# POOL's order of low parts, the place of the router's product on PE, and layer norm statistics by one bn_stats of two tiles

## The chip, the cores and the metric

The kernel runs on one core of a Trainium2 chip. The metric is the device time of one execution in microseconds (us). Engines: PE is TensorE (matmuls; PEld its weight loads), DVE is VectorE, ACT is ScalarE, POOL is GpSimd, SP is SyncE, which here only issues DMAs.

## The reference, cut to what matters

x has 32 batch rows of 512 tokens by 256 channels, all float32. Each row r has six modulation vectors of 256 numbers (sa, ca, ga, sb, cb, gb), made from a conditioning vector.

```python
h = layernorm(x) * (1 + ca) + sa                 # over the 256 channels, eps 1e-5
S = scan over tokens: s = a * s + (1 - a) * h    # a = sigmoid(decay), by channel
x = x + ga * (S @ W.T + b + conv5(h) + conv_b)   # conv5: five taps along tokens, by channel
h = layernorm(x) * (1 + cb) + sb
sel = argmax(gelu(h[:, -1] @ Wp1 + bp1) @ Wp2 + bp2)         # one of 8 experts a row
g = gelu(h @ W1[sel] + b1[sel])
x = x + gb * (h + 0.3 * ((g @ W2[sel] + b2[sel]) @ Wo + bo))
```

## The kernel before, in words

**Tiles.** A row is held as 4 tiles of 128 tokens by 256 channels (`xr`), or, transposed, as 2 tiles of 128 channels by 512 tokens (h, S, rT, hid). The hidden layer of the expert has 4 quarters of 128 features by 512 tokens (g, with f = 0 to 3). For accuracy every large product is made of three: the activation is split into a rounded high part (ACT: `S_hi`, `hid_hi`, `g_hi`) and the remaining low part (POOL: `S_lo`, `hid_lo`, `g_lo`, each one 128x512 subtraction), and the weights likewise; PE does low weight times high part, high times high, high times low part. The products with the high part stand ahead of the product with the low part (`mix`, lines 918, 919, 922; `down`, lines 953, 954, 958; `up`, lines 938 to 940).

**Order.** There is no planner. Each engine has its own list of work, written out by hand as `slot(i)` for i = -3 to 32, and engines meet only by semaphores. An engine does its list strictly in order, so a wait holds up all that stands behind it. Slot i works on four rows at once: row i is in its expert (up, gelu, down), row i+1 in its second norm, hid and router, row i+2 in its mix, convolution and residual, row i+3 in its first norm, h, scan and split of S, and DVE and POOL do the statistics of row i+4. All parts are there in slots 0 to 28 (POOL's and DVE's part for row i+4 in slots up to 27). Setup fills slots -3 to -1: the 8 experts' tables are made there.

**PE's list in a slot** (line 981): mix (line 909) of row i+2, transposes of the slot before's result (line 970), up 0, up 1, transposes of xn, down 0, the first half of up 2, the router's product `nav` (line 1008: four one-column matmuls with Wp1), the second half of up 2, transposes of row i+3 (line 978), the router's logits (lines 1020, 1021), down 1, up 3, transposes of row i+2's residual, down 2, down 3.

**ACT's list** (line 575): two normalisations (line 512; the first writes into S's buffer once both S_lo are made), gelu 0, g_hi 0, gelu 1, g_hi 1 (lines 552, 559), hid (617), hid_hi (625), the router's gelu (634), which waits for PE's nav, rT (572), gelu 2, h (647), g_hi 2, S_hi 0 (546), gelu 3, g_hi 3, S_hi 1, hid_gated (683).

**POOL's list** (line 443): rstd and nmr of the second norm (lines 420, 422), g_lo 0, g_lo 1 (434), gbeta (457), hid_lo (466), rstd and nmr of the first norm of row i+4, g_lo 2, g_lo 3, S_lo 0, S_lo 1 (442).

**DVE's list** (line 784): the expert's result (792), convolution (754, ten instructions) with the last residual in between (803), statistics of row i+4 (`stats1`: four bn_stats, line 704, four bn_aggr, 708, then -mean, 711, and variance + eps, 712), the argmax (832, 834), the scan (781, two), the first residual and statistics of row i+2 (762, 766, 770, 773, 774).

Of the kernel before, what the change touches and what calls it, by code (L numbers as in the profile page):

```python
# [5 lines left out]
def adaln_attention_ffn_kernel(nc, x, decay_logit, W, b, conv_w, conv_b, Wp1, bp1, Wp2, bp2,  # L6
# [16 lines left out]
    ALU = mybir.AluOpType  # L23
    ACT = mybir.ActivationFunctionType

    P = 128
    B, T, D = x.shape
# [4 lines left out]
    TT = T // P  # L32
    DC = D // P
    FC = F // P
    TPB = 512 // D
    HB = TT // TPB
    NX = 6
    NMOD = 6 * D // 512
    EPS = 1e-5
    OUT_SCALE = 0.3  # L40
    GATE_MIN = 0.25

# [19 lines left out]
    with ExitStack() as ctx:  # L62
        def sb(name, shape, dt=f32):
            return ctx.enter_context(nc.sbuf_tensor(name, shape, dt))
# [4 lines left out]
        def sem(name):  # L69
            return ctx.enter_context(nc.semaphore(name))  # L70
# [25 lines left out]


        xr = sb("xr", [P, NX, TT, D])
        st1 = sb("st1", [P, TT, 6])
        mv1 = sb("mv1", [P, TT, 2])  # L100
        ve1 = sb("ve1", [P, TT])
        nm1 = sb("nm1", [P, TT])
        rstd1 = sb("rstd1", [P, TT])
        nmr1 = sb("nmr1", [P, TT])
        st2 = sb("st2", [P, TT, 6])
        mv2 = sb("mv2", [P, TT, 2])
        ve2 = sb("ve2", [P, TT])
        nm2 = sb("nm2", [P, TT])
        rstd2 = sb("rstd2", [P, TT])
        nmr2 = sb("nmr2", [P, TT])  # L110
        xn = sb("xn", [P, TT, D])
# [106 lines left out]
        stored = [sem("stored0"), sem("stored1")]  # L218
        up_loaded = [sem("up_loaded0"), sem("up_loaded1")]
        down_loaded = [sem("down_loaded0"), sem("down_loaded1")]  # L220
        st1_step = sem("st1_step")
        aggr1 = sem("aggr1")
        stats1_ready = sem("stats1_ready")
        rstd1_step = sem("rstd1_step")
        norm1_ready = sem("norm1_ready")
# [9 lines left out]
        r1_ready = sem("r1_ready")  # L235
        t2_done = sem("t2_done")
        x1_ready = sem("x1_ready")
        st2_step = sem("st2_step")
        aggr2 = sem("aggr2")
        stats2_ready = sem("stats2_ready")  # L240
        rstd2_step = sem("rstd2_step")
        norm2_ready = sem("norm2_ready")
# [38 lines left out]
        def wait(eng, s, v):  # L281
            if v > 0:
                eng.wait_ge(s, v)

        def row(r):
            return 0 <= r < B
# [121 lines left out]
        def _(pool):  # L408
# [4 lines left out]
            nc.gpsimd.affine_select(out=ident[:, :], in_=ident[:, :], compare_op=ALU.not_equal, fill=1.0,  # L413
                                    base=0, pattern=[[-1, P]], channel_multiplier=1).then_inc(s_const, 1)

            def norm(r, stats_ready, used, nm, ve, rstd, nmr, step, ready):

                pool.wait_ge(stats_ready, r + 1)
                wait(pool, used, TT * r)
                nc.gpsimd.tensor_tensor(rstd[:, :], ve[:, :], minus_half[:, :], ALU.pow).then_inc(step, 1)  # L420
                pool.wait_ge(step, r + 1)
                nc.gpsimd.tensor_tensor(nmr[:, :], nm[:, :], rstd[:, :], ALU.mult).then_inc(ready, 1)  # L422

            def w1_lo(e):
                pool.wait_ge(s_w1_hi, e + 1)
# [8 lines left out]
                nc.gpsimd.tensor_tensor(g_lo[:, f], g[:, f % 2], g_hi[:, f].bitcast(f32), ALU.subtract).then_inc(g_lo_ready, 1)  # L434

            def norm1(r):
                norm(r, stats1_ready, xn1_ready, nm1, ve1, rstd1, nmr1, rstd1_step, norm1_ready)

            def s_low(r, c):
                wait(pool, mix_done, DC * r)  # L440
# [2 lines left out]

            def slot(i):
                if row(i + 1):
                    norm(i + 1, stats2_ready, xn2_ready, nm2, ve2, rstd2, nmr2, rstd2_step, norm2_ready)
                if i == -3:
                    w1_lo(0)
                if i == -1:
                    w1_lo(5)  # L450
                if row(i):
                    g_low(i, 0)
                    g_low(i, 1)

                    wait(pool, hid_gated_ready, DC * i)
                    pool.wait_ge(up_loaded[i % 2], 16 * (i // 2 + 1))
                    nc.gpsimd.tensor_tensor(gbeta[:, :], up_w[:, i % 2, U_BETA:UPW].bitcast(f32), mods[:, GB:GB + DC, i],
                                            ALU.mult).then_inc(gbeta_ready, 1)
                if row(i + 1):
                    r = i + 1  # L460
                    wait(pool, up_done, FC * (r - 1))
                    if r == 0:
                        pool.wait_ge(s_split_out[0], 32)
                    for c in range(DC):
                        pool.wait_ge(hid_hi_ready, DC * r + c + 1)
                        nc.gpsimd.tensor_tensor(hid_lo[:, r % 2, c], hid_at[r % 2][:, c], hid_hi[:, r % 2, c].bitcast(f32),
                                                ALU.subtract).then_inc(hid_lo_ready, 1)
                if i == -2:
                    w1_lo(3)
                if row(i + 4):  # L470
                    norm1(i + 4)
                if i == -1:
                    w1_lo(6)
                    w1_lo(7)
                if row(i):
                    g_low(i, 2)
                    g_low(i, 3)
                if row(i + 3):
                    s_low(i + 3, 0)
                    s_low(i + 3, 1)  # L480
                if i == -3:
                    w1_lo(1)
                    w1_lo(2)
                if i == -2:
                    w1_lo(4)
# [204 lines left out]
        def _(dve):  # L690
# [7 lines left out]
            dve.wait_ge(s_keep, 1)  # L698
            nc.vector.tensor_scalar(fresh[:, :], keep[:, :], -1.0, 1.0, ALU.mult, ALU.add).then_inc(s_fresh, 1)

            def stats1(r):
                dve.wait_ge(x_loaded[r % NX], 16 * (r // NX + 1))
                for j in range(TT):
                    nc.vector.bn_stats(st1[:, j], xr[:, r % NX, j]).then_inc(st1_step, 1)  # L704
                wait(dve, norm1_ready, r)
                dve.wait_ge(st1_step, TT * (r + 1))
                for j in range(TT):
                    ins = nc.vector.bn_aggr(mv1[:, j], st1[:, j])  # L708
                ins.then_inc(aggr1, 1)
                dve.wait_ge(aggr1, r + 1)  # L710
                nc.vector.tensor_scalar_mul(nm1[:, :], mv1[:, :, 0], -1.0)  # L711
                nc.vector.tensor_scalar_add(ve1[:, :], mv1[:, :, 1], EPS).then_inc(stats1_ready, 1)  # L712

            def mods_setup():

                dve.wait_ge(s_modT, 1)
                view = Q[1][:, 0:6 * DC * B].rearrange("p (m r) -> p m r", r=B)
                nc.vector.tensor_copy(mods[:, SA:SA + DC], view[:, SA:SA + DC])
                nc.vector.tensor_scalar_add(mods[:, CA:CA + DC], view[:, CA:CA + DC], 1.0).then_inc(s_mods1, 1)
                nc.vector.tensor_copy(mods[:, SB:SB + DC], view[:, SB:SB + DC])  # L720
                nc.vector.tensor_scalar_add(mods[:, CB:CB + DC], view[:, CB:CB + DC], 1.0)
                for q, m in enumerate((GA, GB)):
                    ins = nc.vector.tensor_copy(gate_raw[:, q], view[:, m:m + DC])
                ins.then_inc(s_dve, 1)
# [33 lines left out]
            def residual1(r):  # L758
                for k in range(HB):
                    ts = slice(k * TPB, (k + 1) * TPB)  # L760
                    dve.wait_ge(t2_done, HB * r + k + 1)
                    nc.vector.tensor_tensor(xr[:, r % NX, ts], xr[:, r % NX, ts], TR[k][:, :].rearrange("p (t d) -> p t d", d=D),
                                            ALU.add).then_inc(x1_ready, 1)
                    dve.wait_ge(x1_ready, HB * r + k + 1)
                    for j in range(k * TPB, (k + 1) * TPB):
                        nc.vector.bn_stats(st2[:, j], xr[:, r % NX, j]).then_inc(st2_step, 1)
                wait(dve, norm2_ready, r)
                dve.wait_ge(st2_step, TT * (r + 1))
                for j in range(TT):
                    ins = nc.vector.bn_aggr(mv2[:, j], st2[:, j])  # L770
                ins.then_inc(aggr2, 1)
                dve.wait_ge(aggr2, r + 1)
                nc.vector.tensor_scalar_mul(nm2[:, :], mv2[:, :, 0], -1.0)
                nc.vector.tensor_scalar_add(ve2[:, :], mv2[:, :, 1], EPS).then_inc(stats2_ready, 1)

            def scan(r):

# [69 lines left out]
        def _(pe):  # L847
# [74 lines left out]
                        ins = mm(Y[e][:, :], mix_w[:, 0, d, es], S_lo[:, d], start=False, stop=(d == DC - 1))  # L922
                    ins.then_inc(mix_done, 1)

            def up(i, f, parts=range(DC)):
                par, n = i % 2, FC * i + f
                if f == 0:
                    pe.wait_ge(up_loaded[par], 16 * (i // 2 + 1))
                    pe.wait_ge(hid_lo_ready, DC * (i + 1))
                if f == 1:  # L930
                    wait(pe, sel_ready, i + 1)
                if f == 3:

                    pe.wait_ge(sel_ready, min(i + 2, B))
                wait(pe, gelu_out, n - 1)
                for c in parts:
                    w = c * F + f * P
                    mm(U[f % 2][:, :], up_w[:, par, UP + w:UP + w + P], hid_hi[:, par, c], start=(c == 0), stop=False)  # L938
                    mm(U[f % 2][:, :], up_w[:, par, w:w + P], hid_hi[:, par, c], start=False, stop=False)  # L939
                    ins = mm(U[f % 2][:, :], up_w[:, par, w:w + P], hid_lo[:, par, c], start=False, stop=(c == DC - 1))  # L940
                if DC - 1 in parts:
                    ins.then_inc(up_done, 1)

            def down(i, f):
                par, n = i % 2, FC * i + f
# [35 lines left out]
            def slot(i):  # L981
# [13 lines left out]
                    expert(e)  # L995
                if row(i):
                    down(i, 0)
                    up(i, 2, (0,))
                if row(i + 1):
                    r = i + 1  # L1000
                    if r == 0:
# [5 lines left out]
                    for c in range(DC):  # L1007
                        ins = mm(U[1][:, 0:1], wp1[:, c], hid_at[r % 2][:, c, T - 1:T], start=(c == 0), stop=(c == DC - 1))
                    ins.then_inc(r_nav, 1)
                if row(i):  # L1010
                    up(i, 2, (1,))
                if row(i + 3):
                    r = i + 3
                    to_channels(r, xn1, xn1_ready, t1_done)
# [52 lines left out]
```

## Time and profile before

| | us |
|---|---|
| median of 3 runs | 711.05 (710.99 to 711.21) |
| the profiled execution | 709.73 |
| its span, first to last instruction | 707.8 |
| PE busy | 657.7 (93% of the span) |
| PEld busy | 517.2 (73%) |
| DVE busy | 599.8 (85%) |
| ACT busy | 567.2 (80%) |
| POOL busy | 466.8 (66%) |

The profiled execution has 1.93 us around its span. A page of the profile gives busy times, the chain of work that ended last, and the costliest groups of instructions. The timelines give single instructions of one engine by start and duration; the square brackets at a row's end give the time in which the engine stood idle before it and what ended that. Records of successive instructions on one engine overlap a little: the step from start to start is what an instruction costs there, the record's end is what others wait for.

### The profile page before, as it was taken

Reading aid. Unit: us, or ns where it says so; the run is one execution under the profiler, and the core shown is the slowest. Engines: PE = TensorE matmul, PEld = TensorE weight load, DVE = VectorE, ACT = ScalarE, POOL = GpSimd, SP = SyncE. Lnnn points to the kernel's source line nnn. Section 1 sums busy time; section 2 is a strip of 40 time slices with the busy share of each in tenths; the row PEclk is TensorE's granted clock in tenths of the full one; section 3 lists DMA queues with packets and bytes.
Section 4 is the critical chain, followed back from the end, with each engine's and each line's share of the span. In section 5 each row is a group of like instructions: output and inputs, shape, how many; then the busy total and the mean of one; then the engine's idle time right before and its main releaser. Section 6 shows DMA issues by size and latency. Waiting matters only on the chain.

```text
span 707.8 us, 11426 instructions
## 1 busy us (share of the span) xinstructions
PE 657.7 (93%) x3431; PEld 517.2 (73%) x3431; DVE 599.8 (85%) x1350; ACT 567.2 (80%) x979; POOL 466.8 (66%) x432
## 2 busy tenths in 40 slices
PE   5869589999999999999999999999999999999896
PEld 2758367777777778777777777777777777777764
DVE  1778759999999999999999999999999999997621
ACT  3766668888888889988888888889888888887753
POOL 1544556776777776666767777777677777776542
PEclk9989989999999999999999999999999999999998
DMA  7996644555555554454554555545445555544451
GB/s 243 334 298 207 190 143 150 175 179 153 176 162 167 179 160 138 156 151 173 178 176 153 164 163 180 178 132 148 160 161 177 179 155 174 155 143 151 145 158 55
DMA packets 55457, 120.60 MB, mean 170 GB/s; under 512 B 5643, under 2 KB 43364, under 8 KB 46180
## 3 DMA queue, kind: packets, MB, share of 16 engines
q1 hardware_dynamic: 51316, 115.12, 51.7%
q10 hardware_dynamic: 4080, 4.75, 2.3%
q8 instruction: 28, 0.46, 0.3%
q14 instruction: 33, 0.27, 0.1%
HBM read 61.12 MB, written 25.19 MB: 122 GB/s over the span
## 4 chain that ended last, share of the span: by engine, by line
DVE 42%; POOL 25%; PE 15%; issue 8%; ACT 6%; DMA 2%; SPq 0%; POOLq 0%; DVEq 0%; ACTq 0%
DVE Y L754 24%; POOL S_lo L442 9%; POOL g_lo L434 9%; DVE st L704 5%; DVE xr L803 4%; POOL rstd L420 4%; DVE nm L711 3%; PE Y L922 2%; POOL nmr L422 2%; PE Q L905 2%; PE U L938 2%; PE U L940 1%; PE U L939 1%; DVE mv L708 1%; DVE S L781 1%
## 5 line engine op out<-in xcount | busy, mean ns | idle before, releaser
L434 POOL TENSOR_TENSOR g_lo<-g,g_hi 128x512 fp32r<-128x512 f32 x128 | 191.2, 1502 | 162.1 <-ACT g_hi L559 156.5
L754 DVE SCALAR_TENSOR_TENSOR Y<-h,taps,Y 128x512 f32<-128x512 f32 x320 | 222.9, 752 | 13.1 <-PE Y L922 10.6
L512 ACT ACTIVATE S<-xr,nmr,rstd 128x256 f32<-128x256 f32 x128 | 66.6, 592 | 63.9 <-POOL S_lo L442 59.4
L938 PE MATMUL U<-hid_hi,up_w 128*128 128x512 f32 x256 | 107.1, 419 | 7.7 <-DMA up_w<-up_table 7.7
L953 PE MATMUL Q<-g_hi,down_w 128*128 128x512 f32 x256 | 109.7, 429 | 0.2
L552 ACT ACTIVATE g<-U,up_w 128x512 f32<-128x512 f32 x128 | 88.6, 692 | 24.9 <-PE U L940 21.7
L940 PE MATMUL U<-hid_lo,up_w 128*128 128x512 f32 x256 | 101.6, 397 | 0.0
L939 PE MATMUL U<-hid_hi,up_w 128*128 128x512 f32 x256 | 101.5, 397 | 0.0
L954 PE MATMUL Q<-g_hi,down_w 128*128 128x512 f32 x256 | 101.2, 395 | 0.0
L420 POOL TENSOR_TENSOR rstd<-ve,minus_half 128x4 f32<-128x4 f32 x64 | 65.3, 1020 | 30.1 <-DVE ve L712 23.0
L781 DVE TENSOR_TENSOR_SCAN S<-keep,h 128x512 f32<-128x512 f32 x64 | 75.9, 1228 | 10.3 <-ACT h L647 10.3
L958 PE MATMUL Q<-g_lo,down_w 128*128 128x512 f32 x256 | 83.7, 408 | 0.7 <-POOL g_lo L434 0.7
L559 ACT CAST g_hi<-g 128x512 fp32r<-128x512 f32 x128 | 80.5, 629 | 3.1
L442 POOL TENSOR_TENSOR S_lo<-S,S_hi 128x512 fp32r<-128x512 f32 x64 | 81.1, 1288 | 1.9 <-ACT S_hi L546 1.9
L512 ACT ACTIVATE xn<-xr,nmr,rstd 128x256 f32<-128x256 f32 x128 | 66.1, 587 | 9.2 <-POOL nmr L422 9.2
L958 PEld LDWEIGHTS Q<-g_lo,down_w 128*128 128x128 f32 x256 | 45.0, 187 | 23.8 <-POOL g_lo L434 14.6
L922 PE MATMUL Y<-S_lo,mix_w 128*128 128x512 f32 x128 | 47.8, 417 | 14.5 <-POOL S_lo L442 14.5
L938 PEld LDWEIGHTS U<-hid_hi,up_w 128*128 128x128 f32 x256 | 48.8, 191 | 16.7 <-DMA up_w<-up_table 8.1
L792 DVE SCALAR_TENSOR_TENSOR rT<-Q,mods,w_raw 128x512 f32<-128x512 f32 x64 | 44.7, 738 | 17.8 <-PE Q L958 17.8
L940 PEld LDWEIGHTS U<-hid_lo,up_w 128*128 128x128 f32 x256 | 48.7, 190 | 11.4
L953 PEld LDWEIGHTS Q<-g_hi,down_w 128*128 128x128 f32 x256 | 48.1, 188 | 9.9 <-ACT g_hi L559 1.0
L939 PEld LDWEIGHTS U<-hid_hi,up_w 128*128 128x128 f32 x256 | 49.0, 191 | 8.7
(129 smaller groups left out, 1335.7 us busy)
## 6 DMA issues: line engine op xcount, KB each, us to landing
up_w<-up_table SPq DMA_DIRECT2D x32, 1027.0 KB, 6.6
down_w<-down_tab SPq DMA_DIRECT2D x32, 1024.0 KB, 8.6
xr<-in_L_attn_x_dram SPq DMA_DIRECT2D x32, 512.0 KB, 3.6
out_dram<-xr SPq DMA_DIRECT2D x64, 256.0 KB, 2.3
w_raw<-in_L_ffn_W_dram SPq DMA_DIRECT2D x7, 512.0 KB, 5.3
xr<-in_L_ffn_W_dram ACTq DMA_DIRECT2D x6, 512.0 KB, 7.7
up_table<-down_w SPq DMA_DIRECT2D x2, 1024.0 KB, 7.1
up_table<-up_w SPq DMA_DIRECT2D x2, 1024.0 KB, 5.4
```

Of the source, the lines that this page charges most:

```text
L420: nc.gpsimd.tensor_tensor(rstd[:, :], ve[:, :], minus_half[:, :], ALU.pow).then_inc(step, 1)
L434: nc.gpsimd.tensor_tensor(g_lo[:, f], g[:, f % 2], g_hi[:, f].bitcast(f32), ALU.subtract).then_inc(g_lo_ready, 1)
L442: nc.gpsimd.tensor_tensor(S_lo[:, c], S[:, c], S_hi[:, c].bitcast(f32), ALU.subtract).then_inc(S_lo_ready, 1)
L512: nc.scalar.activation(to[:, j], xr[:, r % NX, j], ACT.Identity, bias=nmr[:, j:j + 1], scale=rstd[:, j:j + 1]).then_inc(ready, 1)
L552: nc.scalar.activation(g[:, f % 2], U[f % 2][:, :], ACT.Gelu, bias=up_w[:, i % 2, U_B1 + f:U_B1 + f + 1].bitcast(f32)).then_inc(gelu_out, 1)
L754: ins = nc.vector.scalar_tensor_tensor(out=Y[c][:, :], in0=h[:, c, k:k + T], scalar=taps[:, c, k:k + 1], in1=Y[c][:, :], op0=ALU.mult, op1 ...
L938: mm(U[f % 2][:, :], up_w[:, par, UP + w:UP + w + P], hid_hi[:, par, c], start=(c == 0), stop=False)
L939: mm(U[f % 2][:, :], up_w[:, par, w:w + P], hid_hi[:, par, c], start=False, stop=False)
L940: ins = mm(U[f % 2][:, :], up_w[:, par, w:w + P], hid_lo[:, par, c], start=False, stop=(c == DC - 1))
L953: mm(Q[c][:, :], down_w[:, par, 1, w:w + P], g_hi[:, f], start=(f == 0), stop=False)
L954: mm(Q[c][:, :], down_w[:, par, 0, w:w + P], g_hi[:, f], start=False, stop=False)
L958: ins = mm(Q[c][:, :], down_w[:, par, 0, w:w + P], g_lo[:, f], start=False, stop=(f == FC - 1))
```

## The change

Four edits. On POOL, S_lo 0 moves from behind g_lo 3 to between g_lo 2 and g_lo 3. On PE, up 2 is no longer in two halves: the router's nav product comes behind the whole of it. On DVE, a bn_stats reads two tiles, interleaved channel by channel: its six outputs (count, mean, count x variance of the even and of the odd elements) are then the statistics of the two tiles, so bn_aggr and the two small tensor_scalars go (in the second norm, lines 766 to 774, as in the first). POOL's `norm` does their work instead: 256 x variance + 256 x eps, and -mean, ahead of the power and the product. Its rstd is therefore 1/16 of the old one, and the factor 16 is put into (1 + ca) and (1 + cb) once in setup.

```diff
@@ POOL
-            def norm(r, stats_ready, used, nm, ve, rstd, nmr, step, ready):
-                pool.wait_ge(stats_ready, r + 1)
+            def norm(r, stats_ready, used, st, rstd, nmr, step, ready):
+                pool.wait_ge(stats_ready, HB * (r + 1))
                 wait(pool, used, TT * r)
-                nc.gpsimd.tensor_tensor(rstd[:, :], ve[:, :], minus_half[:, :], ALU.pow).then_inc(step, 1)
-                pool.wait_ge(step, r + 1)
-                nc.gpsimd.tensor_tensor(nmr[:, :], nm[:, :], rstd[:, :], ALU.mult).then_inc(ready, 1)
+                nc.gpsimd.tensor_scalar(rstd[:, :], st[:, :, 2], D * EPS, None, ALU.add).then_inc(step, 1)
+                nc.gpsimd.tensor_scalar(nmr[:, :], st[:, :, 1], -1.0, None, ALU.mult)
+                pool.wait_ge(step, 2 * r + 1)
+                nc.gpsimd.tensor_tensor(rstd[:, :], rstd[:, :], minus_half[:, :], ALU.pow).then_inc(step, 1)
+                pool.wait_ge(step, 2 * r + 2)
+                nc.gpsimd.tensor_tensor(nmr[:, :], nmr[:, :], rstd[:, :], ALU.mult).then_inc(ready, 1)
@@ POOL, slot
                 if row(i):
                     g_low(i, 2)
+                if row(i + 3):
+                    s_low(i + 3, 0)
+                if row(i):
                     g_low(i, 3)
                 if row(i + 3):
-                    s_low(i + 3, 0)
                     s_low(i + 3, 1)
@@ DVE
+            def pair_stats(st, r, k):
+                pair = xr[:, r % NX, k * TPB:(k + 1) * TPB].rearrange("p t d -> p d t")
+                return nc.vector.bn_stats(st[:, k * TPB:(k + 1) * TPB].rearrange("p t s -> p (t s)"), pair)
+
             def stats1(r):
                 dve.wait_ge(x_loaded[r % NX], 16 * (r // NX + 1))
-                for j in range(TT):
-                    nc.vector.bn_stats(st1[:, j], xr[:, r % NX, j]).then_inc(st1_step, 1)
                 wait(dve, norm1_ready, r)
-                dve.wait_ge(st1_step, TT * (r + 1))
-                for j in range(TT):
-                    ins = nc.vector.bn_aggr(mv1[:, j], st1[:, j])
-                ins.then_inc(aggr1, 1)
-                dve.wait_ge(aggr1, r + 1)
-                nc.vector.tensor_scalar_mul(nm1[:, :], mv1[:, :, 0], -1.0)
-                nc.vector.tensor_scalar_add(ve1[:, :], mv1[:, :, 1], EPS).then_inc(stats1_ready, 1)
+                for k in range(HB):
+                    pair_stats(st1, r, k).then_inc(stats1_ready, 1)
...
-                nc.vector.tensor_scalar_add(mods[:, CA:CA + DC], view[:, CA:CA + DC], 1.0).then_inc(s_mods1, 1)
+                nc.vector.tensor_scalar(mods[:, CA:CA + DC], view[:, CA:CA + DC], ROOT_D, ROOT_D, ALU.mult, ALU.add).then_inc(s_mods1, 1)
...
+                    if k == 0:
+                        wait(dve, norm2_ready, r)
                     dve.wait_ge(x1_ready, HB * r + k + 1)
...
+                    pair_stats(st2, r, k).then_inc(stats2_ready, 1)
@@ PE, slot
                 if row(i):
                     down(i, 0)
-                    up(i, 2, (0,))
+                    up(i, 2)
                 if row(i + 1):
...
                         ins = mm(U[1][:, 0:1], wp1[:, c], hid_at[r % 2][:, c, T - 1:T], start=(c == 0), stop=(c == DC - 1))
                     ins.then_inc(r_nav, 1)
-                if row(i):
-                    up(i, 2, (1,))
```

## Rows read from the trace of the kernel before

**Rows 1.** The page: busy time, granted clock by slice, and the chain by engine.

```profile
PE 657.7 (93%) x3431; PEld 517.2 (73%) x3431; DVE 599.8 (85%) x1350; ACT 567.2 (80%) x979; POOL 466.8 (66%) x432
...
PEclk9989989999999999999999999999999999999998
...
DVE 42%; POOL 25%; PE 15%; issue 8%; ACT 6%; DMA 2%; SPq 0%; POOLq 0%; DVEq 0%; ACTq 0%
```

**Rows 2.** Waits from 300 to 500 us: us in total, times, longest us.

```profile
POOL g_lo L434 <- ACT g_hi L559: 44.4, 10, 4.5
ACT S L512 <- POOL S_lo L442: 23.2, 11, 2.3
...
PE Y L922 <- POOL S_lo L442: 5.3, 11, 0.6
PEld Q L958 <- POOL g_lo L434: 5.0, 12, 0.4
```

**Rows 3.** Timeline of PE in one slot: start us, duration us, line and operation.

```profile
633.41 0.50 PE L922 MATMUL Y<-S_lo,mix_w 128*128 128x512 f32 x1 [0.48 <-POOL S_lo L442]
633.75 0.39 PE L918 MATMUL Y<-S_hi,mix_w 128*128 128x512 f32 x1
633.98 0.39 PE L919 MATMUL Y<-S_hi,mix_w 128*128 128x512 f32 x1
...
638.56 0.39 PE L940 MATMUL U<-hid_lo,up_w 128*128 128x512 f32 x1
...
641.76 0.58 PE L1008 MATMUL U<-w_raw,wp 128*128 128x1 f32 x4
642.20 0.48 PE L938 MATMUL U<-hid_hi,up_w 128*128 128x512 f32 x1
...
649.04 0.73 PE L958 MATMUL Q<-g_lo,down_w 128*128 128x512 f32 x2
649.61 0.39 PE L953 MATMUL Q<-g_hi,down_w 128*128 128x512 f32 x1
...
650.55 0.63 PE L958 MATMUL Q<-g_lo,down_w 128*128 128x512 f32 x2
651.01 0.39 PE L918 MATMUL Y<-S_hi,mix_w 128*128 128x512 f32 x1
...
651.93 0.39 PE L922 MATMUL Y<-S_lo,mix_w 128*128 128x512 f32 x1
652.78 0.50 PE L922 MATMUL Y<-S_lo,mix_w 128*128 128x512 f32 x1 [0.46 <-POOL S_lo L442]
```

**Rows 4.** Timeline of ACT in the same slot.

```profile
638.99 0.69 ACT L552 ACTIVATE g<-U,up_w 128x512 f32<-128x512 f32 x1
...
642.61 0.26 ACT L634 ACTIVATE nav<-U,vecs 128x1 f32<-128x1 f32 x1
...
645.99 0.65 ACT L559 CAST g_hi<-g 128x512 fp32r<-128x512 f32 x1
```

**Rows 5.** Timelines of POOL and DVE in the same slot.

```profile
646.78 3.45 POOL L434 TENSOR_TENSOR g_lo<-g,g_hi 128x512 fp32r<-128x512 f32 x2 [1.92 <-ACT g_hi L559]
650.20 2.53 POOL L442 TENSOR_TENSOR S_lo<-S,S_hi 128x512 fp32r<-128x512 f32 x2
...
645.56 2.34 DVE L781 TENSOR_TENSOR_SCAN S<-keep,h 128x512 f32<-128x512 f32 x2 [0.83 <-ACT h L647]
```

**Rows 6.** Timeline of POOL: g_lo 3 of that slot by itself.

```profile
648.95 1.28 POOL L434 TENSOR_TENSOR g_lo<-g,g_hi 128x512 fp32r<-128x512 f32 x1
```

**Rows 7.** Timelines of DVE and POOL in a slot with first norm; its PE starts at 361.82.

```profile
370.41 1.40 DVE L704 BATCH_NORM_STATS2 st<-xr 128x6 f32<-128x256 f32 x4
372.33 0.97 DVE L711 TENSOR_SCALAR nm<-mv 128x4 f32<-128x4 f32 x1
...
370.74 2.54 POOL L466 TENSOR_TENSOR hid_lo<-w_raw,hid_hi 128x512 fp32r<-128x512 f32 x2 [0.40 <-ACT hid_hi L625]
374.54 0.65 POOL L422 TENSOR_TENSOR nmr<-nm,rstd 128x4 f32<-128x4 f32 x1
375.19 3.46 POOL L434 TENSOR_TENSOR g_lo<-g,g_hi 128x512 fp32r<-128x512 f32 x2
```

**Rows 8.** POOL's small instructions: duration ns min/median/max, first and last start us.

```profile
L420 POOL TENSOR_TENSOR rstd<-ve,minus_half x64: 997/1007/1846, 12.7 to 669.9; 128x4 f32<-128x4 f32 x64
L422 POOL TENSOR_TENSOR nmr<-nm,rstd x64: 198/200/942, 13.8 to 671.0; 128x4 f32<-128x4 f32 x64
```

**Rows 9.** Timeline of PE: the first stall of this kind, and a gap near the end.

```profile
109.78 0.50 PE L922 MATMUL Y<-S_lo,mix_w 128*128 128x512 f32 x1 [0.46 <-POOL S_lo L442]
...
671.19 1.09 PE L970 MATMUL Q<-ident,rT 128*128 128x128 f32 x8 [1.78 <-DVE rT L792]
```

More of the change, by code:

```diff
@@ L39, in adaln_attention_ffn_kernel @@
     EPS = 1e-5
+    ROOT_D = 16.0
+    assert ROOT_D * ROOT_D == D
     OUT_SCALE = 0.3
@@ L98, in adaln_attention_ffn_kernel @@
         xr = sb("xr", [P, NX, TT, D])
[L99 to L102, printed above, removed]
+        st1 = sb("st1", [P, TT, 3])
         rstd1 = sb("rstd1", [P, TT])
         nmr1 = sb("nmr1", [P, TT])
[L105 to L108, printed above, removed]
+        st2 = sb("st2", [P, TT, 3])
         rstd2 = sb("rstd2", [P, TT])
@@ L220, in adaln_attention_ffn_kernel @@
         down_loaded = [sem("down_loaded0"), sem("down_loaded1")]
-        st1_step = sem("st1_step")
-        aggr1 = sem("aggr1")
         stats1_ready = sem("stats1_ready")
@@ L237, in adaln_attention_ffn_kernel @@
         x1_ready = sem("x1_ready")
-        st2_step = sem("st2_step")
-        aggr2 = sem("aggr2")
         stats2_ready = sem("stats2_ready")
@@ L436, in norm1 @@
             def norm1(r):
-                norm(r, stats1_ready, xn1_ready, nm1, ve1, rstd1, nmr1, rstd1_step, norm1_ready)
+                norm(r, stats1_ready, xn1_ready, st1, rstd1, nmr1, rstd1_step, norm1_ready)
             def s_low(r, c):
@@ L445, in slot @@
                 if row(i + 1):
-                    norm(i + 1, stats2_ready, xn2_ready, nm2, ve2, rstd2, nmr2, rstd2_step, norm2_ready)
+                    norm(i + 1, stats2_ready, xn2_ready, st2, rstd2, nmr2, rstd2_step, norm2_ready)
                 if i == -3:
@@ L718, in mods_setup @@
                 nc.vector.tensor_copy(mods[:, SA:SA + DC], view[:, SA:SA + DC])
-                nc.vector.tensor_scalar_add(mods[:, CA:CA + DC], view[:, CA:CA + DC], 1.0).then_inc(s_mods1, 1)
+                nc.vector.tensor_scalar(mods[:, CA:CA + DC], view[:, CA:CA + DC], ROOT_D, ROOT_D, ALU.mult, ALU.add).then_inc(s_mods1, 1)
                 nc.vector.tensor_copy(mods[:, SB:SB + DC], view[:, SB:SB + DC])
-                nc.vector.tensor_scalar_add(mods[:, CB:CB + DC], view[:, CB:CB + DC], 1.0)
+                nc.vector.tensor_scalar(mods[:, CB:CB + DC], view[:, CB:CB + DC], ROOT_D, ROOT_D, ALU.mult, ALU.add)
                 for q, m in enumerate((GA, GB)):
@@ L763, in residual1 @@
                                             ALU.add).then_inc(x1_ready, 1)
+                    if k == 0:
+                        wait(dve, norm2_ready, r)
                     dve.wait_ge(x1_ready, HB * r + k + 1)
[L765 to L774, printed above, removed]
+                    pair_stats(st2, r, k).then_inc(stats2_ready, 1)
             def scan(r):
@@ L923, in mix, with up @@
                     ins.then_inc(mix_done, 1)
-            def up(i, f, parts=range(DC)):
+            def up(i, f):
                 par, n = i % 2, FC * i + f
@@ L935, in up @@
                 wait(pe, gelu_out, n - 1)
-                for c in parts:
+                for c in range(DC):
                     w = c * F + f * P
@@ L940, in up @@
                     ins = mm(U[f % 2][:, :], up_w[:, par, w:w + P], hid_lo[:, par, c], start=False, stop=(c == DC - 1))
-                if DC - 1 in parts:
-                    ins.then_inc(up_done, 1)
+                ins.then_inc(up_done, 1)
             def down(i, f):
```

## Prediction, made before the changed kernel was run

> **What bounds the kernel now.** I start with busy shares: PE is busy 93% of the span, DVE 85%, ACT 80%, POOL 66%, and the clock is granted in full through the middle [rows 1]. The kernel repeats one slot. PE's stall for S_lo 1 stands at 109.78, the same stall 28 slots later at 652.78 [rows 3, 9]: 543.00 / 28 = 19.39 us a slot. So I look for what fixes 19.39.
>
> The chain of waits names DVE (42%) and POOL (25%) [rows 1], the engines from which the change takes work or which it reorders. The waits tell more: PE waits only for POOL's low parts (5.3 us in 11 waits for S_lo, its weight loads 5.0 us for g_lo), POOL waits for ACT's g_hi, and ACT waits 2.1 us a slot for S_lo [rows 2]. The deciding view is the slot from 633.41 to 652.78. It is slot 28, where no row is left for DVE's first statistics and POOL's first norm. It still lasts 19.37 us. Here POOL stands idle 1.92 us and then starts g_lo 2 on ACT's g_hi, 646.78 - 633.41 = 13.37 us after PE's start [rows 3, 5]. In the slot with statistics and norm, g_lo 2 starts at 375.19 - 361.82 = 13.37 us [rows 7]. The two paths are equally long, and taking the statistics away altogether gave nothing.
>
> So the other loop sets the slot: PE (mix to up 1) to ACT's gelu 1 at 638.99, which starts 0.04 after the record of up 1's last matmul ends (638.56 + 0.39) [rows 3, 4]; ACT's list to g_hi 2; POOL's four low parts; PE.
>
> **Part 1, nav behind the whole of up 2.** Nav now starts at 641.76, behind three matmuls of up 2 [rows 3]. Behind six it starts 3 x 0.23 = 0.69 later, at 642.45 (the step of 0.23 is 633.75 to 633.98). Its four take 0.58, so they end at 643.03, and ACT can start the router's gelu 0.04 later, at 643.07, where it now starts at 642.61 [rows 4], as soon as hid_hi is done. That is +0.46 us, and behind it on ACT stand rT, gelu 2, h, g_hi 2, S_hi, with no idle time up to g_hi 2's end at 645.99 + 0.65 = 646.64 [rows 4]. g_hi 2 ends at 647.10. The cover that nav had was hid_hi, and it ran out 0.27 us after nav's end (642.34 to 642.61). PE itself gains about 0.1: the first matmul behind nav costs 642.52 - 642.20 = 0.32 in place of 0.23, and this goes; PE has waits behind it, so I count nothing. Logits still come behind the transposes and reach DVE when they do now; so the table's DMAs start as now. The up 2 result is ready earlier, but gelu 2 stands behind rT on ACT.
>
> **Part 2, statistics.** DVE loses, of its first statistics, four bn_aggr and two small instructions: from the end of bn_stats (370.41 + 1.40 = 371.81) to 373.30, 1.5 us, and of the second nearly 0.9. One bn_stats of 512 elements should cost a little less than two of 256 (estimate: 4 x 0.33 = 1.32 becomes 1.2). I count all of this at nothing, because in slots 0 to 27 POOL cannot start the first norm before hid_lo ends, 370.74 + 2.54 = 373.28, and now starts it at 373.45 [rows 7]. POOL gains 0.17 us there and pays for two more instructions and one more semaphore step. The nearest row to a tensor_scalar of 128x4 is the product nmr, 0.20 us; the farthest is the power, 1.01 [rows 8]. I take 0.2 each plus 0.1. This is hidden: today g_lo 2 starts 375.19 - 373.28 = 1.91 us behind hid_lo's end [rows 7], with ACT's delay from Part 1 2.37, and the work is 0.4 + 0.1 + 1.0 + 0.1 + 0.2 = 1.8. At 1.0 each it is 3.4, and 1.0 us a slot would show. At the low end the cost is nothing.
>
> Nmr took 0.65 in place of 0.20 [rows 7, 8] while DVE's scan ran. Scan 0 spans 373.97 to 375.14, and nmr ends at 375.19. The Trainium skill (SBUF — State Buffer, Who interferes with whom) says that a DVE instruction with two SBUF inputs and a GpSimd instruction that reads SBUF lock each other out for a whole instruction. The trace agrees for nmr; g_lo 2, begun in scan 1, would by that rule end 1.28 behind the scan, at 647.90 + 1.28 = 649.18, and it ended at 648.95. The sum would be the same by either, since scan and g_lo 2 move together. By the same rule DVE's two small tensor_scalars, which go, were waits for POOL and not work (0.97 us [rows 7]). So an earlier start of the norm doesn't bring nmr ahead of scan 0's end, and scan 0 hangs on ACT's h (0.83 us idle before it [rows 5]), which Part 1 moves by 0.46.
>
> **Part 3, S_lo 0 between g_lo 2 and g_lo 3.** Today: g_lo 2 at 646.78, g_lo 3 from 648.95 to 650.23 [rows 5, 6], S_lo 0 and 1 to 652.73; PE picks up S_lo 1 at 652.78 [rows 3]. Before its two waits PE has: g_lo 2 at 649.04, g_lo 3 at 650.55 without a wait, S_lo 0 at 651.93 without a wait [rows 3]. So S_lo 0 was never late. In the new order g_lo 3 comes 1.27 us later, and PE needs it 1.38 us before S_lo 0.
>
> In numbers, with all three parts, in this slot's times. PE's start isn't a stall any more, so its first step is 0.23 instead of 0.34 (633.41 to 633.75): everything behind it is 0.11 earlier. g_lo 2 starts at 646.78 + 0.46 - 0.11 = 647.13. It takes 648.95 - 646.78 = 2.17, since the scan beside it moves with it: 649.30. S_lo 0, 1.27: 650.57. g_lo 3, 1.28: 651.85. PE starts down 3's low product 0.05 later, 651.90, in place of 650.55. Then two of them after a stall, 0.57 (649.04 to 649.61), four high products of mix, 0.92 (651.01 to 651.93), S_lo 0's product, 0.23, and S_lo 1's at 653.62. POOL has ended S_lo 1 by 653.12, so there is no stall left there. Start to start that is 653.62 - 633.41 = 20.21 in place of 19.37: **+0.84 us a slot**. Of this 0.46 is nav; the order alone gives 0.38: the stall of 0.6 for S_lo 1 goes, and a longer one for g_lo 3 stands ahead of it.
>
> **Sum.** S's low parts and g's stand together in slots 0 to 28: 29 x 0.84 = 24.4. Setup: POOL's norm is 0.5 longer on a path that ends at the tables, DVE's statistics at about 44 us shorter: net 0 (bounds -1 to +1). Tail, slots 29 to 31: PE waits 1.78 us for DVE at 671.19 [rows 9], behind the second statistics; it gets about 0.5 of it back, and loses 0.3 to the router's wait twice: net 0. Span 707.8 + 24.4 = 732.2; with the 1.93 us around it the profiled execution would show 734.1. The median of the runs is 1.32 above the profiled one's 709.73, so 711.05 + 24.4 = **735.5**.
>
> **Rivals.**
> A. *The DVE–POOL loop is the bound* (what the chain of waits says at face value). DVE gives back 1.6 us in the first norm's path, POOL pays 0.5: 1.1 a slot, 29 x 1.1 = 32, 679. The end of it is PE without any stall: 19.37 less 0.85 - 0.23 and 0.11 at S_lo, 0.27 at g_lo 2, 0.09 in up 2 is 18.3, the same amount. It decides from the point where POOL's start of g_lo 2 doesn't hang on ACT. Against it stands slot 28. Chance 0.08.
> B. *Nav is absorbed*, because ACT finds idle time that the overlapping records hide. Then +0.38 a slot, 29 x 0.38 = 11: 722. Chance 0.10.
> C. *The small POOL instructions cost as much as the power*: +1.0 a slot more in slots 0 to 27, 28 us: 763; at 0.6 each the norm takes 2.6, 0.2 more a slot, 741. Chance 0.08.
> D. *Nothing comes of it*: g_lo 2 gets shorter, since the lock no longer falls on it (0.89 of its 2.17 is beyond the plain 1.28), and this pays for nav and for the order (0.84). It needs the scan to be done before g_lo 2, against the row above. 711, chance 0.04.
> The forecast has 0.69, its own range 729 to 741 (0.65 to 1.05 a slot).
>
> **Chances.** What can be told from no change here is 0.2%, 1.4 us. Faster: A's 0.08 and 0.01 for what lies between A and D: 0.09. Same: D, 0.04. Slower: forecast, B and C, 0.69 + 0.10 + 0.08 = 0.87. The range for 8 in 10 takes in the forecast, most of B and the low half of C: 720 to 745.
>
> **What would show it.** Right: PE's idle at the mix's S_lo gone and 1 to 1.5 us of it at down 3's low product, waiting for g_lo; ACT's router gelu shows idle time of about 0.4 us that PE's nav ends; DVE busy falls by some 75 us without use; a slot of 20.2. Wrong: a slot under 19.4, or ACT's gelu of the router starting right at hid_hi's end. If POOL's waits for g_hi 2 are gone while g_lo 2 starts late, C is at work.

## Result: slower by 2.6%, and the profile after

| | before | after |
|---|---|---|
| median of 4 runs, us | 711.02 (710.91 to 711.21) | 729.62 (728.78 to 731.16) |
| ratio | 1 | 1.0262, 95% interval 1.0247 to 1.0276 |
| profiled execution / its span, us | 709.73 / 707.8 | 730.42 / 728.5 |

The forecast was 735.5 with a range of 720 to 745, so 24.4 us were forecast and 18.6 came. The profiled executions differ by 20.7 us, the medians by 18.6: the one of before was 1.3 below its median, the one of after 0.8 above.

The page after, parts 1 and 4, answers to [rows 1]:

```profile
PE 657.9 (90%) x3431; PEld 523.7 (72%) x3431; DVE 532.0 (73%) x838; ACT 570.0 (78%) x979; POOL 495.1 (68%) x560
...
PE 53%; ACT 14%; issue 13%; POOL 9%; DVE 6%; DMA 3%; SPq 0%; ACTq 0%; POOLq 0%; DVEq 0%
```

DVE is busy for 67.8 us less and nothing came of it. POOL took on 28 us. The chain of waits has moved from DVE to PE.

Waits from 300 to 500 us, to be read beside [rows 2]:

```profile
PEld Q L946 <- POOL g_lo L430: 21.8, 20, 1.3
...
DVE S L770 <- ACT h L645: 13.4, 10, 1.3
...
PE Q L946 <- POOL g_lo L430: 13.0, 20, 0.8
...
ACT nav L632 <- PE U L996: 2.9, 10, 0.3
```

PE no longer waits for S_lo. It waits for g_lo, twice a slot. A new wait stands on ACT: 10 times 0.29 us for nav. One slot on PE, then on ACT, then on POOL:

```profile
381.26 0.50 PE L996 MATMUL U<-w_raw,wp 128*128 128x1 f32 x4
...
388.22 0.73 PE L946 MATMUL Q<-g_lo,down_w 128*128 128x512 f32 x2 [0.49 <-POOL g_lo L430]
...
390.71 0.73 PE L946 MATMUL Q<-g_lo,down_w 128*128 128x512 f32 x2 [0.83 <-POOL g_lo L430]
391.28 0.39 PE L907 MATMUL Y<-S_hi,mix_w 128*128 128x512 f32 x1
...
392.21 0.62 PE L911 MATMUL Y<-S_lo,mix_w 128*128 128x512 f32 x2
```

```profile
381.80 0.26 ACT L632 ACTIVATE nav<-U,vecs 128x1 f32<-128x1 f32 x1 [0.30 <-PE U L996]
...
385.17 0.65 ACT L557 CAST g_hi<-g 128x512 fp32r<-128x512 f32 x1
```

```profile
383.72 0.23 POOL L413 TENSOR_SCALAR rstd<-st 128x4 f32<-128x4 f32 x1
384.03 0.23 POOL L414 TENSOR_SCALAR nmr<-st 128x4 f32<-128x4 f32 x1
384.23 1.04 POOL L416 TENSOR_TENSOR rstd<-rstd,minus_half 128x4 f32<-128x4 f32 x1
385.34 0.62 POOL L418 TENSOR_TENSOR nmr<-nmr,rstd 128x4 f32<-128x4 f32 x1
385.96 2.21 POOL L430 TENSOR_TENSOR g_lo<-g,g_hi 128x512 fp32r<-128x512 f32 x1
388.13 1.30 POOL L438 TENSOR_TENSOR S_lo<-S,S_hi 128x512 fp32r<-128x512 f32 x1
389.38 1.28 POOL L430 TENSOR_TENSOR g_lo<-g,g_hi 128x512 fp32r<-128x512 f32 x1
390.61 1.30 POOL L438 TENSOR_TENSOR S_lo<-S,S_hi 128x512 fp32r<-128x512 f32 x1
```

and on DVE:

```profile
384.74 2.34 DVE L770 TENSOR_TENSOR_SCAN S<-keep,h 128x512 f32<-128x512 f32 x2 [1.34 <-ACT h L645]
```

Read from the end: both products with S_lo are taken without a stall (x2, 0.62 together), S_lo 0 having been ready since 389.43, 2.8 us early, and S_lo 1 since 391.91. The 0.83 us stall stands ahead of them, at down 3's low product, for g_lo 3, which S_lo 0 has pushed back by one instruction. The 0.49 us stall at down 2's is for g_lo 2. It starts at 385.96, 0.14 behind the end of g_hi 2, the same distance as in the slot without a norm (646.64 to 646.78). POOL's own nmr ends at 385.96 too: it took 0.62 us beside DVE's scan, which had waited for ACT's h. So two waits end together there, and both hang on ACT's list, which is late because its router gelu began at 381.80, 0.04 behind the end of nav. The clock is granted in full through the slots (1.00 from 100 to 120 us), as before.

A slot is taken from here on from nav in slot 0 to nav in slot 28:

```profile
99.87 0.50 PE L996 MATMUL U<-w_raw,wp 128*128 128x1 f32 x4
...
662.66 0.50 PE L996 MATMUL U<-w_raw,wp 128*128 128x1 f32 x4
```

562.79 / 28 = 20.10 us. Before, the same two stand at 98.75 and 641.76: 19.39. So 28 x 0.71 = 19.8 of the 20.7 us lie in these slots.

### The profile page after: what moved, and what is told of

The parts are those of the page before. It is cut to its first block, busy times and chain, and to the rows that moved or that the text cites. A ratio compares the mean times of both kernels' runs of the same rounds, so it can differ in the third digit from the quotient of the medians.

```text
span 728.5 us, 11042 instructions
## 1 busy us (share of the span) xinstructions
PE 657.9 (90%) x3431; PEld 523.7 (72%) x3431; DVE 532.0 (73%) x838; ACT 570.0 (78%) x979; POOL 495.1 (68%) x560
## 4 chain that ended last, share of the span: by engine, by line
PE 53%; ACT 14%; issue 13%; POOL 9%; DVE 6%; DMA 3%; SPq 0%; ACTq 0%; POOLq 0%; DVEq 0%
PE U L927 6%; PE U L929 6%; PE U L928 6%; ACT g L550 6%; POOL g_lo L430 6%; PE Q L946 5%; DVE S L770 5%; PE Y L907 4%; PE Y L908 4%; PE Q L958 4%; PE Y L911 4%; PE TR L966 4%; ACT g_hi L557 3%; ACT h L645 3%; PE Q L941 2%
## 5 line engine op out<-in xcount | busy, mean ns | idle before, releaser
L946 PE MATMUL Q<-g_lo,down_w 128*128 128x512 f32 x256 | 86.8, 420 | 38.5 <-POOL g_lo L430 38.5
L927 PE MATMUL U<-hid_hi,up_w 128*128 128x512 f32 x256 | 104.5, 408 | 7.7 <-DMA up_w<-up_table 7.7
L928 PE MATMUL U<-hid_hi,up_w 128*128 128x512 f32 x256 | 101.7, 397 | 0.0
L946 PEld LDWEIGHTS Q<-g_lo,down_w 128*128 128x128 f32 x256 | 42.7, 187 | 71.8 <-POOL g_lo L430 65.1
L702 DVE BATCH_NORM_STATS2 st<-xr 128x6 f32<-128x512 f32 x128 | 87.5, 705 | 7.4 <-DMA xr<-in_L_attn_x_dram 3.0
L438 POOL TENSOR_TENSOR S_lo<-S,S_hi 128x512 fp32r<-128x512 f32 x64 | 82.6, 1292 | 1.9 <-ACT S_hi L544 1.9
L416 POOL TENSOR_TENSOR rstd<-rstd,minus_half 128x4 f32<-128x4 f32 x64 | 66.4, 1037 | 0.0
```

Of the source, the lines that this page charges most:

```text
L946: ins = mm(Q[c][:, :], down_w[:, par, 0, w:w + P], g_lo[:, f], start=False, stop=(f == FC - 1))
```

## Experiments

In every case "slot" is nav to nav over these 28 slots. Intervals are of the ratio to the kernel before on the same chip, worked out over all the runs, so a ratio need not be the quotient of two medians. The median of before was 711.80 beside nav_only, order_only, stats_only and nav_back, 710.79 beside stats_again, dve_low1 and dve_low01, 710.75 beside g2_first_act and g2_first_both, 710.95 beside order_back and dve_low1_late.

| run | nav | order | statistics | slot, us | median, us | ratio (95% interval) |
|---|---|---|---|---|---|---|
| before | | | | 19.39 | 711.02 | 1 |
| nav_only | new | | | 19.78 | 723.58 | 1.0161 (1.0139 to 1.0183) |
| order_only | | new | | 19.71 | 720.84 | 1.0134 (1.0113 to 1.0154) |
| stats_only | | | new | 19.38 | 708.08 | 0.9948 (0.9931 to 0.9966) |
| stats_again | | | new | 19.39 | 708.74 | 0.9968 (0.9956 to 0.9980) |
| nav_back | | new | new | 19.73 | 718.58 | 1.0103 (1.0079 to 1.0127) |
| order_back | new | | new | 19.77 | 720.8 | 1.0139 (1.0120 to 1.0158) |
| after | new | new | new | 20.10 | 729.62 | 1.0262 (1.0247 to 1.0276) |

**nav_only**, the kernel before with this alone:

```diff
-                    up(i, 2, (0,))
+                    up(i, 2)
...
-                if row(i):
-                    up(i, 2, (1,))
```

> The kernel before with the router's product behind the whole of up 2, nothing else. Theory (one loop PE - ACT - POOL - PE sets the slot, ACT's router gelu hangs on nav's end): ACT's router gelu starts about 0.37 us later in every slot (nav starts 0.69 later, its four take 0.50 instead of 0.58), g_lo 2 with it, and nothing makes up for it: 29 x 0.37 = 11 us, 722. The parts add up, so that this and the order's share together give the whole change. Rival (the order alone carries the loss, nav is absorbed by slack on ACT): within 2 us of 711.

723.58, slot +0.39. PE waits for g_lo 2 and S_lo 1, and ACT's row (the second fence) has a wait for nav that before did not have:

```profile
364.48 0.73 PE L958 MATMUL Q<-g_lo,down_w 128*128 128x512 f32 x2 [0.49 <-POOL g_lo L434]
...
368.22 0.50 PE L922 MATMUL Y<-S_lo,mix_w 128*128 128x512 f32 x1 [0.47 <-POOL S_lo L442]
...
377.27 0.50 PE L1008 MATMUL U<-w_raw,wp 128*128 128x1 f32 x4
```

```profile
377.81 0.26 ACT L634 ACTIVATE nav<-U,vecs 128x1 f32<-128x1 f32 x1 [0.29 <-PE U L1008]
```

The theory holds: the four take 0.50 behind six matmuls of up 2, in place of 0.58. ACT's router gelu starts 377.81 - 368.22 = 9.59 us behind PE's start of the slot, where it was 642.61 - 633.41 = 9.20 [rows 3, 4]: 0.39 late, and the slot with it.

**order_only**, POOL's edit alone:

```diff
                     g_low(i, 2)
+                s_low(i + 3, 0)
                     g_low(i, 3)
-                s_low(i + 3, 0)
                 s_low(i + 3, 1)
```

> The kernel before with S_lo 0 between g_lo 2 and g_lo 3 on POOL, nothing else. Theory: PE's stall for S_lo 1 (0.6 us) goes and one for g_lo 3 of about 0.9 us comes ahead of it; 0.38 us a slot, 29 x 0.38 = 11 us, 722. Rival (the order is harmless, nav carries the loss): within 2 us of 711. Rival 2 (the order costs the whole delay of g_lo 3, 1.27 us a slot): 748.

720.84, slot +0.32, near the theory's 722 and far from both rivals, 711 and 748. PE's stall for S_lo is gone and this one has come; below it g_lo 2 on POOL in this slot and the next:

```profile
366.04 0.73 PE L960 MATMUL Q<-g_lo,down_w 128*128 128x512 f32 x2 [0.84 <-POOL g_lo L434]
```

```profile
361.28 2.21 POOL L434 TENSOR_TENSOR g_lo<-g,g_hi 128x512 fp32r<-128x512 f32 x1
...
381.02 2.21 POOL L434 TENSOR_TENSOR g_lo<-g,g_hi 128x512 fp32r<-128x512 f32 x1
```

**stats_only**, DVE's and POOL's statistics alone.

> The kernel before with the statistics by one bn_stats of two tiles and POOL's longer norm, nothing else. Theory: the DVE - POOL loop and the PE - ACT - POOL loop are equally long, so DVE's 2.5 us a slot bring nothing: 710 to 712, POOL's g_lo 2 still starts 13.4 us after PE's start of the slot, on ACT's g_hi 2. Rival (DVE was the bound): 1.1 us a slot less, 680. Rival 2 (POOL's two more instructions cost): up to 0.4 us a slot more, 720.

708.08: the slot did not change (19.38), as expected, so both rivals are out. But the time fell by 3.7 us (from 711.80) where 0 was expected. So it ran again.

> The statistics alone once more, with more rounds, because 3.7 us less came where 0 was expected, while its slot got only 0.02 us shorter (19.38 against 19.39 us over 28 slots, 0.5 us). Theory (the gain lies outside the slots, in setup and tail, where DVE's statistics stand on the path): again 2 to 5 us less, at 707 to 709. Rival (chance of that chip and day): within 1 us of the kernel before.

708.74, ratio 0.9968: a gain of 2.1 us by the medians and 2.3 by the ratio, beyond the noise, and outside the slots (19.39). PE waited for rT in setup 6.72 us before and 5.87 now (the first row below). But this is lost again at the expert tables' DMA, behind which slot 0 starts: at 90.74 us before, at 91.42 in stats_only and 90.63 in stats_again; over all profiles of this study that start lies between 89.5 and 92.7. At the start of slot 30 PE waits for DVE's result 1.78 us before [rows 9] and 1.76 in nav_only and order_only, but 1.36 to 1.37 in all ten profiles with the new statistics. These 0.41 us are a gain.

What else differs between the profiles is the clock. Behind the wait for the tables PE starts slot 0 at the lower of its two levels (granted 0.50, 1.2 GHz) and a matmul takes a step of 0.43 us instead of 0.23. Before, this lasts to about 95.2; in stats_again it ends at 93.36 (the second row), and nav of slot 0 stands at 97.82 instead of 98.75; in stats_only, where it lasts longer, at 99.53. The last transposes took 1.68 us before, at a granted clock of 0.53 from 703 to 704, and 1.09 in stats_only and stats_again, at 1.00. Whether the statistics have a part in this, and where the rest of the 2.1 us comes from, stays open.

```profile
50.42 1.94 PE L957 MATMUL TR<-ident,rT 128*128 128x128 f32 x8 [5.87 <-ACT rT L568]
...
93.36 0.48 PE L925 MATMUL U<-hid_hi,up_w 128*128 128x512 f32 x1
```

**nav_back** is the changed kernel with nav in its old place, **order_back** the changed kernel with POOL's old order.

> The changed kernel with the router's product put back between the halves of up 2; order and statistics stay changed. Theory: the delay of ACT goes, the order's 0.38 us a slot stays: 722 (18 us over 711 less 0.35 x 29 = 10 gives 720). Rival (nav matters only because the order is changed or the other way round): 711 or 729.

> The changed kernel with S_lo 0 put back behind g_lo 3; nav and statistics stay changed. Theory (the parts add): 708.5 for the statistics alone and 11.5 for nav: 720. The order's share is the rest to 729.6, 9.6. Rival (nav's delay only bites with g_lo 3 late): 712.

718.58 and 720.8, both as their theories had it. By slots nav costs 0.39 alone, 0.37 on top of the other two and 0.39 on top of the statistics; the order 0.32, 0.33 and 0.35. The parts add up to within 0.03 us.

**S_lo 1 on DVE.** If the slot ends with POOL's row of low parts, the idle time that the statistics left on DVE can be used. These three runs keep nav in its old place and have the new statistics. POOL leaves out what DVE takes over, and makes the rest behind g_lo 3 as before; each half of S_lo has a semaphore of its own (not shown). In the cut, `DVE_LOW` is (1,) or, in dve_low01, (0, 1):

```diff
+            def s_low(r, c):                     # DVE
+                if c in DVE_LOW and row(r):
+                    wait(dve, mix_done, DC * r)
+                    dve.wait_ge(S_hi_ready, DC * r + c + 1)
+                    nc.vector.tensor_tensor(S_lo[:, c], S[:, c], S_hi[:, c].bitcast(f32), ALU.subtract).then_inc(S_lo_ready[c], 1)
...
                                             ALU.add).then_inc(x1_ready, 1)
+                    s_low(r + 1, k)              # dve_low1, dve_low01
                     if k == 0:
                         wait(dve, norm2_ready, r)
                     dve.wait_ge(x1_ready, HB * r + k + 1)
                     pair_stats(st2, r, k).then_inc(stats2_ready, 1)
+                s_low(r + 1, 1)                  # dve_low1_late: here instead
```

> Statistics changed, order and nav as before, and S_lo 1 made by DVE instead of POOL, behind the second residual add. Theory (the slot is a loop through POOL's four low parts, with DVE's new idle time outside it): PE's stall for S_lo 1 (0.62 and 0.11 of restart) goes, 0.73 us a slot, 29 x 0.73 = 21 us: 687. Rival (shared port: DVE's instruction with two SBUF inputs waits for POOL's or holds it up): DVE gets in only behind S_lo 0, a third or half of the gain, 695 to 700. Rival 2 (ACT's path alone sets the slot and POOL's end of it doesn't matter): 708.

> As the other, with both S_lo 0 and S_lo 1 made by DVE. Theory: no wait of PE for S_lo, as there, 687, and no more, since PE's work without waits is 18.3 to 18.6 us a slot. Rival (shared port): g_lo 3 is held up by DVE's S_lo 0, or S_lo 0 waits for g_lo 2, up to 0.6 us a slot worse than the other, 687 to 704.

> S_lo 1 by DVE as in the run at 692.9 us, but behind DVE's last statistics instead of ahead of them, where it met POOL's S_lo 0 (which took 1.74 us instead of 1.28) and cost PE a stall of 0.08 and a restart of 0.11. Theory (lock on the shared port; who starts first has it for the instruction): POOL's S_lo 0 is now first and takes 1.28, DVE's waits for it and ends when PE is about to need it: 0 to 0.19 us a slot less, 687 to 693. Rival (no lock, the 1.74 has another cause): 692.9 and S_lo 0 still at 1.74.

dve_low1: 692.9 us, ratio 0.9747 (0.9726 to 0.9767), slot 18.81. dve_low01: 698.54, ratio 0.9829 (0.9807 to 0.9852), slot 18.94. dve_low1_late: **688.78 us, ratio 0.9695 (0.9672 to 0.9717)**, slot 18.68; it beats both kernels. In dve_low1 PE's stall for S_lo 1 is gone, but the time lies between the theory's 687 and the rival's 695 to 700: POOL's S_lo 0, stretched to 1.74, took a part of the gain, as dve_low1_late shows. dve_low01's time is within the rival's 687 to 704. POOL's S_lo 0 in dve_low1, and DVE's S_lo 1 beside it:

```profile
369.95 1.74 POOL L439 TENSOR_TENSOR S_lo<-S,S_hi 128x512 fp32r<-128x512 f32 x1
```

```profile
369.55 1.00 DVE L758 TENSOR_TENSOR S_lo<-S,S_hi 128x512 fp32r<-128x512 f32 x1
```

In dve_low1_late POOL's starts first:

```profile
368.50 1.29 POOL L439 TENSOR_TENSOR S_lo<-S,S_hi 128x512 fp32r<-128x512 f32 x1
```

```profile
368.85 1.50 DVE L758 TENSOR_TENSOR S_lo<-S,S_hi 128x512 fp32r<-128x512 f32 x1
```

Whoever starts second pays, and PE needs S_lo 0 before S_lo 1. The time is where the theory had it, 687 to 693, and POOL's subtraction is back from 1.74 to 1.29, against the rival. In dve_low01 POOL's g_lo 2 and g_lo 3 together took 3.92 us instead of 3.47, which fits the rival, the shared port.

**g_hi 2 ahead of h.** On top of dve_low1, ACT makes g_hi 2 directly behind gelu 2 (g2_first_act), and in the second run POOL also makes g_lo 2 ahead of the first norm (g2_first_both):

```diff
                     gelu(i, 2)                   # ACT, both
+                    g_high(i, 2)
...
-                    g_high(i, 2)                 # from behind h
@@ POOL, g2_first_both alone
+                    g_low(i, 2)
                     norm1(i + 4)
-                    g_low(i, 2)
```

> S_lo 1 by DVE as in the run at 692.9 us, and on ACT g_hi 2 directly behind gelu 2, ahead of h. Theory (g_lo 2 hangs on ACT's g_hi 2, and the norm on POOL is done early): g_hi 2 1.3 us earlier, but the norm's last instruction now meets DVE's scan, which is 0.6 later, and is locked out until scan 0 ends; g_lo 2 starts 0 to 0.6 later than before, 693 to 705. Rival (no lock in the way, g_lo 2 0.4 us earlier): the stall before down 2's low product (0.27) goes, 685.

> As the other, and on POOL g_lo 2 ahead of the first norm. Theory (the loop PE - ACT - POOL ends at g_lo 2; the norm isn't needed before the next slot): g_lo 2 starts on g_hi 2, 1.3 us earlier, PE's stall at down 2's low product goes, 0.3 us a slot, and S_lo 0's too: 18.81 to 18.45 us, 29 x 0.36 = 10 us, 682. Rival (h, the scan and S_hi are 0.6 later, and PE waits for S_lo 1 on DVE instead): 693 or more.

713.22 (ratio 1.0032, 1.0019 to 1.0045; slot 19.46) and 734.27 (1.0329, 1.0309 to 1.0349; slot 20.19). The first went the way of the theory, further than its range (693 to 705): nmr took 0.88 us, and g_lo 2 started 359.33 - 353.69 = 5.64 us behind nav where it was 5.01, 0.63 later, and the slot is 0.65 longer. The second expectation was wrong. g_lo 2 did start early, but the norm then stood beside DVE's scan; rows of POOL, then of DVE:

```profile
366.06 1.29 POOL L431 TENSOR_TENSOR g_lo<-g,g_hi 128x512 fp32r<-128x512 f32 x1 [0.73 <-ACT g_hi L557]
367.44 1.03 POOL L414 TENSOR_SCALAR rstd<-st 128x4 f32<-128x4 f32 x1
368.54 1.03 POOL L415 TENSOR_SCALAR nmr<-st 128x4 f32<-128x4 f32 x1
...
370.80 1.28 POOL L431 TENSOR_TENSOR g_lo<-g,g_hi 128x512 fp32r<-128x512 f32 x1
```

```profile
366.70 2.85 DVE L777 TENSOR_TENSOR_SCAN S<-keep,h 128x512 f32<-128x512 f32 x2 [1.50 <-ACT h L647]
```

Two instructions of 0.23 us took 1.03 each, the scans 2.85 instead of 2.34, and g_lo 3 started 8.58 us behind nav (362.22), where in dve_low1 it had ended by 8.48, so PE waited 0.50 us for that, behind a wait of 0.43 for g_hi 3, which ACT makes behind S_hi 0 and so behind the scan. What was left out was the place of the scan beside each instruction that moved.

## Why the prediction was right

**The bound.** Right: slot 28, which lasts as long without statistics as with them, said that DVE was not the only bound. stats_only (slot 19.38) shows it, and rival A, the chain at face value, is out. The signs came too, two of them smaller than forecast: ACT's router gelu waits 0.30 for nav (0.4 forecast), and DVE's busy time fell by 67.8 us without use (75). At down 3's low product PE's record shows 0.83 us idle (1 to 1.5 forecast); by steps, 390.71 where 389.49 + 0.23 = 389.72 was possible, it is 0.99.

**Part 1, nav.** Right in kind, too large: +0.46 forecast, 0.37 to 0.39 measured. The term that was mis-sized is nav's four matmuls, taken at 0.58 as [rows 3] have them; behind the whole of up 2 they take 0.50. Why they are shorter there no run tells. Rival B, nav absorbed, is out by nav_only.

**Part 2, statistics.** Right in the slot: the two new instructions cost 0.23 each (0.2 forecast) and are hidden, DVE's time is not used. Two bn_stats of 512 elements take 1.32, where four of 256 took 1.40 [rows 7]. Rival C is out here, though g2_first_both shows its price, 1.03 each, as soon as they stand beside the scan. The prediction put the 0.97 us of DVE's small tensor_scalar down to the rule for two SBUF inputs. That instruction has one, so the rule as told there does not cover it; it ends at 373.30, 0.02 behind POOL's hid_lo [rows 7], which fits a wait and does not show more. Wrong outside the slots: setup and tail were counted at net 0 (bounds -1 to +1), and the statistics alone brought 2.1 us there in the run of twelve and 3.7 in the run of four. Of that, 0.41 is shown, in the tail (0.5 forecast).

**Part 3, the order.** Right, and its steps nearly to the hundredth: for the order alone they give 19.37 + 0.38 = 19.75 us, and the slot shown above lasts 381.02 - 361.28 = 19.74. Over 28 slots the mean is 19.71, and the mean of before is 19.39, where slot 28, my base, has 19.37: so the mean rise is 0.32. Rival D is out: from g_lo 2 to the next start on POOL it is 2.17 us (385.96 to 388.13), as before.

**The sum.** I forecast a slot of 20.21. Less 0.08 for nav it is 20.13; the slot shown lasts 390.71 - 370.59 = 20.12 (PE's stall for g_lo 3 to the next), the mean is 20.10, the rise of the mean 0.71. 29 x 0.84 = 24.4 was forecast, 29 x 0.71 = 20.6 is what these sizes leave, and the profiled executions differ by 20.7. The medians differ by 18.6, because the two profiled executions lie on the outer sides of their medians. If the slots grew alike in all executions, which only the profiled ones show, the ends are 2.0 us shorter by the medians. That is as much as stats_again alone gave (2.1), and the term that the sum had at 0. In the two profiles themselves it does not show: 20.7 is 0.1 more than the slots give.

## What to carry to other kernels

A stall that a consumer shows last (here S_lo) is not helped by making that operand earlier if another operand of the same producer is consumed before it: write down the consumer's order of need, and let the producer follow it. A slot in which part of the work is missing, such as the last one, is a free experiment on what bounds the others. Work taken from an engine off the bound pays only once something from the bound is put in its place: the statistics brought 0.3 to 0.5%, the same with S_lo 1 moved into the gap 3.1%. No run moves S_lo 1 to DVE with the old statistics, so how much of the 3.1% needs them is not shown.

## What the runs showed of the hardware

DVE's scan or its S_lo subtraction, which read two SBUF operands each, and a POOL instruction stretch each other, down to the smallest: POOL's 128x4 tensor_scalar took 0.23 us alone and 1.03 beside the scan; POOL's 128x512 subtraction 1.28 alone, 1.74 beside DVE's S_lo 1 and 2.21 beside scan 1; DVE's S_lo subtraction 0.68 alone (in dve_low01), 1.50 when POOL's started first. The Trainium skill (SBUF — State Buffer, Who interferes with whom) has the one that starts second wait for the whole of the other's instruction. These rows agree nearly. In dve_low1_late POOL's S_lo 0 ends at 369.79, and DVE's ends at 370.35, 0.56 behind it, where a step of it alone takes 0.61 (in dve_low01). In dve_low1 POOL's g_lo 3 ends at 370.00, DVE's S_lo 1 at 370.55, and POOL's S_lo 0 at 371.69, 0.14 less than 1.28 behind that. Beside the scan the loser gets off 0.2 us more lightly than by the rule, as the prediction saw on g_lo 2.
